# The scale of LayerNorm in the softmax's exponent, and a reordered first block, in a gated cross-attention and SwiGLU kernel

## The reference

```python
def _layernorm(x, axis=-1, eps=1e-05):
    m = jnp.mean(x, axis=axis, keepdims=True)
    v = jnp.var(x, axis=axis, keepdims=True)
    return (x - m) / jnp.sqrt(v + eps)
...
q, k, v = heads(query @ Wq.T), heads(key @ Wk.T), heads(value @ Wv.T)   # 16 heads of 32
scores = jnp.einsum('bhqd,bhkd->bhqk', q, k) * HD ** -0.5
scores = jnp.where(causal[None, None], scores, -1e9)
out = jnp.einsum('bhqk,bhkd->bhqd', jax.nn.softmax(scores, axis=-1), v)
...
x = x + jnp.tanh(g_xattn[0]) * xattn(_layernorm(x), ctx, ctx, Wq, Wk, Wv, Wo)
x = x + jnp.tanh(g_ffn[0]) * ffn(_layernorm(x), w_gate, w_up, w_down)
return x
```

## Time and profile before

| | us |
|---|---|
| median of 3 runs | 894.29 |
| lowest and highest | 893.69, 894.61 |
| the profiled execution: its own time | 893.84 |
| its span, first to last instruction | 892.0 |
| PE busy | 858.7 |
| DVE busy | 655.2 |
| ACT busy | 439.6 |
| POOL busy | 437.0 |

### The profile page before, as it was taken

One profiled execution on the slowest core, in us unless ns is written; L12 is line 12 of the kernel. 1 busy time (PEld: TensorE's weight loads), 2 busy tenths in 40 slices (PEclk: granted clock), 3 DMA queues, 4 the chain that ended last, 5 costly groups with the idle time before them and its releaser, 6 DMA issues.

```text
span 892.0 us, 12923 instructions
## 1 busy us (share of the span) xinstructions
PE 858.7 (96%) x4089; PEld 708.5 (79%) x4089; DVE 655.2 (73%) x1082; ACT 439.6 (49%) x1130; POOL 437.0 (49%) x372
## 2 busy tenths in 40 slices
PE   4979999999999999999999999999999999999997
PEld 2758888888888878778888888888888888888876
DVE  3777868685868697759878758698487787487782
ACT  2566646555565656546326446055364165361450
POOL 5375767675767665338324615144444146141250
PEclk9999999999999999999999999999999999999999
DMA  6526364555556531537614336333256133243212
GB/s 202 152 63 202 126 206 140 189 168 162 167 163 199 190 123 54 205 120 281 227 41 154 113 120 240 113 115 139 88 195 241 37 129 131 89 157 144 83 42 96
DMA packets 61845, 129.53 MB, mean 145 GB/s; under 512 B 8672, under 2 KB 21472, under 8 KB 61792
## 3 DMA queue, kind: packets, MB, share of 16 engines
q1 hardware_dynamic: 61504, 128.85, 42.6%
q10 hardware_dynamic: 288, 0.00, 0.0%
HBM read 100.72 MB, written 27.80 MB: 144 GB/s over the span
## 4 chain that ended last, share of the span: by engine, by line
PE 79%; POOL 6%; DVE 6%; ACT 4%; issue 3%; DMA 1%; SPq 0%; ACTq 0%; POOLq 0%; DVEq 0%
PE psum L1723 34%; PE psum L1475 24%; PE psum L1773 18%; POOL xs L561 4%; PE psum L1509 3%; POOL e L575 2%; ACT e L791 1%; PE psum L1590 1%; ACT pT L762 1%; DMA wq_stage<-wq_t 1%; DVE pT L1017 1%; DVE den L1071 1%; POOL hT L697 1%; DVE aT L1033 1%; ACT aT L779 1%
## 5 line engine op out<-in xcount | busy, mean ns | idle before, releaser
L1723 PE MATMUL psum<-xv,ring 128*128 128x512 f32 x1344 | 308.0, 390 | 0.9 <-ACT a L934 0.7
L1723 PEld LDWEIGHTS psum<-xv,ring 128*128 128x128 f32 x1344 | 251.3, 188 | 55.1 <-ACT a L934 1.1
L697 POOL TENSOR_TENSOR hT<-th,hT 128x512 fp32r<-128x512 f32 x48 | 86.7, 1806 | 200.7 <-ACT hT L954 200.7
L1773 PE MATMUL psum<-w_d,hT 128*128 128x512 f32 x768 | 177.7, 390 | 1.3 <-POOL hT L697 0.8
L1773 PEld LDWEIGHTS psum<-w_d,hT 128*128 128x128 f32 x768 | 143.6, 188 | 32.7 <-POOL hT L697 2.0
L575 POOL TENSOR_TENSOR e<-e,rden 128x616 f32<-128x616 f32 x64 | 78.0, 1220 | 103.4 <-DVE rden L1073 77.0
L1475 PE MATMUL psum<-xT,wq 128*128 128x512 f32 x384 | 95.6, 402 | 3.5 <-POOL xT L567 2.9
L1475 PE MATMUL psum<-wo,aT 128*128 128x512 f32 x384 | 95.4, 398 | 0.5 <-DVE aT L1033 0.5
L1355 DVE SCALAR_TENSOR_TENSOR acc<-psum,gate_ffn,acc 128x512 f32<-128x512 f32 x64 | 47.6, 749 | 65.1 <-PE psum L1773 65.1
L922 ACT ACTIVATE a<-psum 128x512 f32<-128x512 f32 x48 | 28.7, 599 | 131.6 <-PE psum L1723 131.4
L1475 PEld LDWEIGHTS psum<-xT,wq 128*128 128x128 f32 x384 | 71.4, 191 | 18.9 <-POOL xT L567 3.1
(11 more groups left out here) (107 smaller groups left out, 1231.4 us busy)
## 6 DMA issues: line engine op xcount, KB each, us to landing
ring<-w_var SPq DMA_DIRECT2D x48, 896.0 KB, 4.6
w_var<-stage SPq DMA_DIRECT2D x12, 896.0 KB, 5.0
x_ln<-x SPq DMA_DIRECT2D x32, 256.0 KB, 4.9
x_res<-x SPq DMA_DIRECT2D x32, 256.0 KB, 5.2
x_mid<-x_res SPq DMA_DIRECT2D x32, 256.0 KB, 2.0
x<-x_mid SPq DMA_DIRECT2D x16, 512.0 KB, 5.6
acc<-x_mid SPq DMA_DIRECT2D x16, 512.0 KB, 6.0
out<-acc SPq DMA_DIRECT2D x32, 256.0 KB, 2.0
```

Source lines behind the costliest of these rows:

```text
L697: nc.gpsimd.tensor_tensor(hT[:, 1, i % HH, j, :], h[:, :], hT[:, 0, i % HH, j, :].bitcast(f32), ALU.subtract).then_inc(h_lo, 1)
L1723: last = nc.tensor.matmul(psum[:, bank, :], stat, mov, start=start and j == 0, stop=j == len(terms) - 1, skip_group_check=not start)
L1773: last = nc.tensor.matmul(m_bank[t % 2][:, :], hT[:, a, m, t // TT, (t % TT) * P:(t % TT + 1) * P], w_d[:, HH * h + m, :], start=m == 0 an ...
```

## The change

Four things are done. `rstd` no longer touches x. It is computed as (HD * var + HD * EPS) ** -0.5, which is LayerNorm's scale times SCALE, and it becomes the `scale` operand of `exp0` and `exp1`, one value per partition, in the place of the constant SCALE; `nmx` is the maximum times the same value, negated. The DMAs to and from `rs_row`, `rsb`, and `x_scale` go, and `x_high_t` waits for the load alone. `exp0` and the first `nmx` of a block wait for `scale_ready`.

Block 0 is formed in the same way: its queries come from `x_t`, so that normalising, transposing and splitting rows of x go. The loads of `xs` and `wq_stage` are issued first, half of them from ACT's queue. 24 products of `ident` with itself (`WARM`) run on PE before the mean of Wq, whose four products now wait each for its own part of Wq.

The program of block 0 on each engine is written anew. PE scores the first unit of tile t + 1 ahead of the second unit of tile t; keys 0 and 1 come before queries 2 and 3. DVE takes the statistics of block 0 there and those of block 1 in place of block 2. Block 1 takes those of blocks 2 and 3, two per place in place of one.

POOL splits the output weights (`wo`) and the values of the second batch after block 0's probabilities. `v_late`, the second half of `v_full`, lies over other memory, and SP therefore waits for `v_split[1]` before it fetches the weights of the second stage and the rows `x_res` of block 1's residual. NEG becomes -1e30.

```diff
-    NEG = -1e9
+    NEG = -1e30
+    WARM = 24
@@ SP @@
-            load_x(0, first=True)
-            for k in range(KD):
-                sp.dma_start(wq_stage[:, k, :], ...)
+            for k in range(KD // 2):
+                sp.dma_start(xs[:, k, :], xt_f[0, :, k, :]).then_inc(xs_in[k], 16)
+            for k in range(KD // 2):
+                sp.dma_start(wq_stage[:, k, :], ...)
             ctx_stage; wk_stage
+            load_x(0, first=True)
             wv_stage
-            sp.wait_ge(t_full, 4)
-            load_x(1, first=True)
+            load_xs(1)
             x_res <- wo_t
-            load_xs(1, first=True)
-            spread_rstd(1, first=True)
+            load_x(1)
...
             load_xs(2)
+            load_x(2)
             sp.wait_ge(wo_split, 2)
+            sp.wait_ge(v_split[1], 1)
             fetch(1, 0)
             fetch(1, 1)
@@ POOL @@
-            def x_scale(n):
-                pool.wait_ge(rsb_in, 16 * n)
-                for k in range(KD):
-                    pool.wait_ge(xs_in[k], 16 * n)
-                    nc.gpsimd.tensor_tensor(xs[:, k, :], xs[:, k, :], rsb[:, :], ALU.mult).then_inc(x_scaled, 1)
+            def variance(n): rstd = mv * HD + HD * EPS
+            def score_scale(n):
+                if not (isinstance(n, int) and n == 0):
+                    pool.wait_ge(exp1_done, 4 * n)
+                pool.wait_ge(var_eps, n + 1)
+                nc.gpsimd.tensor_tensor(q_scale[:, :], rstd[:, :], half[:, :], ALU.pow).then_inc(scale_ready, 1)
+            variance(0); score_scale(0)
+            x_low_t(1, (0, 1)); probabilities(0, 0); x_low_t(1, (2, 3))
+            probabilities(0, 1); probabilities(0, 2); probabilities(0, 3)
+            variance(1); score_scale(1)
+            wo low parts, then v_low_rows(1)
             def block(n, ahead, first=False):
                 probabilities(n, 0)
-                x_scale(n + 1)
                 x_low_t(n + 1, (0, 1))
...
                 probabilities(n, 3)
+                score_scale(n + 1)
                 if ahead:
-                    rstd1(n + 2)
+                    variance(n + 2)
@@ ACT @@
+            for k in range(KD // 2, KD):
+                act.dma_start(xs[:, k, :], xt_f[0, :, k, :]).then_inc(xs_in[k], 16)
+            for k in range(KD // 2, KD):
+                act.dma_start(wq_stage[:, k, :], ...)
             def x_high_t(n, k):
-                act.wait_ge(x_scaled, 4 * (n - 1) + k + 1)
+                act.wait_ge(xs_in[k], 16 * n + 16)
-                nc.scalar.activation(e[:, t % 2, 0:UH, :], ..., ACT.Exp, scale=SCALE)
+                nc.scalar.activation(e[:, t % 2, 0:UH, :], ..., ACT.Exp, scale=q_scale[:, t:t + 1])
-                        bias=nmx[:, t % 2, h:h + 1], scale=SCALE, accum_out=...)
+                        bias=nmx[:, t % 2, h:h + 1], scale=q_scale[:, t:t + 1], accum_out=...)
+            first_block(): exp0(0, 0) query0(3) x_high_t(1, 0..3) wo_high(0) exp1(0, 0) exp0(0, 1)
+                p(0, 0) p(0, 1) exp1(0, 1) p(0, 2) wo_high(1) exp0(0, 2) p(1, 0) exp1(0, 2) p(1, 1)
+                p(1, 2) exp0(0, 3) q(0) p(2, 0) exp1(0, 3) q(1) p(2, 1) p(2, 2) v_high(0) q(2) ...
@@ DVE @@
+            x_low_t(0..3); centre and wq_low in turn; query0(0) query0(1) k_low(0) k_low(1)
+            stats(0, 0..3); query0(2)
+            first_block(): shift0(0, 0) k_low(2) k_low(3) query0(3) denominator0(0, 0) shift0(0, 1)
+                shift1(0, 0) denominator1(0, 0) v_copy(0) denominator0(0, 1) p(0, 0) shift1(0, 1) p(0, 1)
+                denominator1(0, 1) p(0, 2) shift0(0, 2) p(1, 0) denominator0(0, 2) v_copy(1) shift1(0, 2)
+                p(1, 1) denominator1(0, 2) p(1, 2) shift0(0, 3) denominator0(0, 3) q(0) p(2, 0)
+                shift1(0, 3) q(1) p(2, 1) stats(1, 0) stats(1, 1) denominator1(0, 3) p(2, 2) q(2)
+                v_low_rows(0) p(3, 0) p(3, 1) stats(1, 2) stats(1, 3) q(3) p(3, 2)
@@ PE @@
+            for _ in range(WARM):
+                nc.tensor.matmul(t_bank[0][:, 0:P], ident[:, :], ident[:, :], start=True, stop=True)
             avg product, each of the four waiting for its own wq_in[k]
+            queries 0 and 1, k by k, each k waiting for w_split k + 1
+            keys(0) keys(1) query(2, 2) keys(2) keys(3)
+            first_block(): unit(0, 0) query(3, 3) unit(1, 0) unit(0, 1) batch_values(0) p(0, 0)
+                unit(1, 1) p(0, 1) p(0, 2) unit(2, 0) p(1, 0) batch_values(1) unit(2, 1) p(1, 1) p(1, 2)
+                unit(3, 0) q(0) p(2, 0) unit(3, 1) q(1) p(2, 1) p(2, 2) q(2) p(3, 0) p(3, 1) q(3) p(3, 2)
```

More of the change, by code:

```diff
@@ L90, in t_base @@
     def t_base(n):
[L91 removed]
+        return 12 * n
     V_AT = 4
@@ L815, in step, with query0 @@
-            def step(n, first, query):
+            for k in range(KD):
+                x_high_t(0, k)
+            for k in range(KD):
+                split_hi(wq_centred, wq[:, 0, k], wq_stage[:, k, :], k + 1)
+            act.wait_ge(gates_in, 32)
+            nc.scalar.activation(gate_t[:, :], gates[:, :], ACT.Tanh).then_inc(gates_tanh, 1)
+            def query0(m):
+                m_high(m, m, qT[:, 0, m, :])
+            query0(0)
+            query0(1)
+            act.wait_ge(k_zero, 1)
@@ new lines, in _, with first_block, p, q @@
+            k_high(0)
+            k_high(1)
+            query0(2)
+            k_high(2)
+            k_high(3)
+            def first_block():
+                def p(t, r):
+                    p_high(0, t, r, 3 * t + r)
+                def q(m):
+                    m_high(M_Q1 + m, m, qT[:, 0, m, :])
+                exp0(0, 0)
+                query0(3)
+                for k in range(KD):
+                    x_high_t(1, k)
+                wo_high(0)
+                exp1(0, 0)
+                exp0(0, 1)
+                p(0, 0)
+                p(0, 1)
+                exp1(0, 1)
+                p(0, 2)
+                wo_high(1)
+                exp0(0, 2)
+                p(1, 0)
+                exp1(0, 2)
+                p(1, 1)
+                p(1, 2)
+                exp0(0, 3)
+                q(0)
+                p(2, 0)
+                exp1(0, 3)
+                q(1)
+                p(2, 1)
+                p(2, 2)
+                v_high(0)
+                q(2)
+                p(3, 0)
+                p(3, 1)
+                q(3)
+                p(3, 2)
+                v_high(1)
@@ L832, in step @@
-                q_at = M_Q1 if first else m_base(n) + 8
+                weighted(0)
+                exp1(n, 0, lambda: weighted(1))
+                weighted(2)
+                weighted(3)
+                if query:
+                    for k in range(KD):
+                        x_high_t(n + 1, k)
+                q_at = m_base(n) + 8
                 def q(m):
@@ new lines, in step @@
+                st(3)
+                if not query:
+                    xv_low(0, B11, b11_at)
+                q(1)
+                q(2)
+                p(3, 0)
+                q(3)
+                p(3, 1)
+                p(3, 2)
+                if not query:
+                    form(0, T1)
+            first_block()
+            step(1, True, True)
+            with dve.Fori(2, NB - 2) as n:
+                step(n, True, True)
+            step(NB - 2, True, False)
+            step(NB - 1, False, False)
```

607 lines of the change are left out of this document (281 added, 326 removed).

## The result

The changed kernel takes 899.26 us (898.39 to 900.95, four runs) against 894.28 for the kernel before: a ratio of 1.0058, with a 95% interval of 1.0046 to 1.0070. The forecast of 899.2 stood on the right side and on the right number. The number came by luck: held against the traces, the sum had the price of the operand 4.5 us too small and everything else 4.7 us too dear, and the two errors cancel.

A forecast was written before the change was run, and what follows sets the result against it. It took block 0 as bound by the chain through the engines, later blocks by PE with one gap. Block 0 +4.5, block 1 +2.6, blocks 2 to 6 -3.0, block 7 +0.8: +4.9, so 899.2 us; range 889.5 to 903.

The forecast's parts named there:

- the gap that goes in the steady blocks: Blocks 2 to 6: PE's 0.92 us wait for a low part before its third round of transposes goes without x_scale.
- the three waits at the end of block 0: Block 0, tiles 2 and 3: PE stands 2.5, 2.4 and 3.0 us before p(2, 0), p(3, 0) and p(3, 1).
- I take 0.05 a piece: ACT's exponentials: the per-partition scale adds 0.05 us each, bounds 0 and 0.08; 0.4 us per exp1.
- I take back 0.3 of the 0.92: Blocks 2 to 6: longer exp1 delays queued copies, leaving 5 x (-0.6) = -3.0 us.
- the 1.28 of the earlier trace: Block 7: a PE wait of 1.28 us behind an exp1, for which the forecast put +0.8 us (0 to +1.2).
- Rival 1: All blocks: the scale operand costs nothing; +0.3 us in all, 894.6 us; chance 0.18.
- 5 x 0.92 = 4.6: Blocks 2 to 6: us saved as the 0.92 us gap goes in each, before the operand's price.
- The walk gives 0.3, 0.5, 0.9 and 1.2 us at four places: Block 1: PE waits from doubled statistics and a late low part of q(3), 4.0 us in all; +2.6 taken.
- the walk: Start and block 0, step by step by engine: block 1's scores at 76.8 us at price zero, 78.5 with 0.05.
- one term of 1.6 us: End of block 0: one loss to PE's lowered clock behind the new gaps, 1.6 us added.
- Rival 3: Last query and block 1's start: clock stays at half, twice the 1.6, operand at 0.08; 903.1 us; chance 0.12.
- Rival 2: Block 0, tiles 2 and 3: queued steps overlap, gaps sum to less than 6 us; 889.6 us; chance 0.27.

The follow-up runs named there:

- experiment 1: The changed kernel with the constant SCALE back as scale of both exponentials, leaving LayerNorm's scale out of the attention's exponent: 890.13 us, 0.9951 of the kernel before.
- experiment 9: The changed kernel with clock-holding products behind Wq's mean, statistics behind the second sum and the copy p(1, 1) ahead of tile 2's exp1: 895.66 us.
- experiment 3: The kernel before with only LayerNorm's scale put into the exponent for blocks 1 to 7, old start and old block 0 kept: 890.81 us, 0.9958.
- experiment 6: The changed kernel with 8 more products of ident behind Wq's mean, while PE waits for centred Wq: 898.30 us, 1.0047 of the kernel before.
- experiment 7: The changed kernel with block 0's second sum and low part p(2, 2) ahead of two statistics of block 1 on DVE: 897.27 us, 1.0037.
- experiment 4: The kernel of experiment 3 with ACT's high parts of block 1's x before the first exp0, POOL's low parts around the first probabilities: 888.58 us, 0.9931.
- experiment 5: The changed kernel without the 24 warm-up products ahead of Wq's mean (WARM = 0): 900.03 us, 1.0056 of the kernel before.

## Why the prediction was right, and where only its sum was

**What held and what was luck.** Right were the side, the gap that goes in the steady blocks, and the three waits at the end of block 0, each in its place. The total was luck: with 0.09 in place of 0.05 the same sum would have had some 4 us more, near 903, at the edge of its range. Of the signs that it named, the mean of the second-half activations was 0.427 (0.39 to 0.40 forecast), their steps 0.39 (0.35), block 1's first scores came at 81.33 (near 80) behind a window at clock 0.51 (0.50), and Wq's mean was done at 12.24 (13.8).

**The operand's size: too small.** The step "I take 0.05 a piece" is wrong: 0.09, above the upper bound of 0.08, and the section "What ACT_TABLE_LOAD costs" of the page "ScalarE: Activation LUTs" of the Trainium skill was right where the bounds from the earlier trace rows were not. These took the length of an activation without an operand from a slope through two other shapes; a group of like activations with the operand and one without it give the price directly (427 and 341 ns).

**Where the operand is paid.** The step "I take back 0.3 of the 0.92" for each steady block put the price where it costs little (0.14 to 0.21 in blocks 2 to 5). It put too little where it is paid: 0.3 in block 6 (measured 1.69), 0.5 in block 1 (1.61), 0.8 in block 7 (1.64), 1.7 in block 0 (3.44). In block 7 it also had the wrong wait: the 1.28 of the earlier trace rows did not grow, those of the scores for `exp1` did. In all the sum had 4.6 us for the operand and the runs show 9.1. Rival 1, the free operand, falls at both ends: the operand is not free, and without it the time is 890.1 and not 894.6.

**Everything else: too dear.** At price zero the sum had +0.3 us, and experiment 1's cuts show -4.4.
- Blocks 2 to 6: "5 x 0.92 = 4.6" is short of the measured 7.1. In block 6 of before two more waits for DVE, of 0.43 and 0.49, stood behind the first, and these go too: 2.26. In the other four 1.2 goes each, where the gap was 0.92; the rest, 0.3, lies within PE's busy time (41.86 before, 41.56 to 41.59 in experiment 1, in blocks 2 and 3). Half of that came with the changed kernel (41.71) and half with the constant scale. What makes PE's busy time longer beside a busier ACT or POOL was not settled.
- Block 1: +2.1 forecast, +0.36 measured. "The walk gives 0.3, 0.5, 0.9 and 1.2 us at four places" was right in its places (0.35, 0.34, 0.87, 0.71 in the kernel after), but half of it comes only together with the operand: experiment 1 keeps 0.35 and 0.70.
- Block 0: +2.8 at price zero with the clock's share, +2.25 measured. The order of the walk held; the terms of the operand, the start and the clock were mis-sized.

**The start.** The mean was done at 12.24, below the range of 12.9 to 15.6, since the warm-up itself ended at 8.8 and not at 10.4. The queries then ended at 21.65 where the walk had 21.4. The gap behind the mean was in the walk (2.1, measured 2.26). What was missed is the clock behind it: the queries took 7.15 us and not 5.5, which took back the 1.6 us that the earlier mean had given.

**The clock** was one term of 1.6 us behind the new gaps. The query behind them lost 1.35 against the 3.00 of the earlier trace rows, another at 63.56, behind the wait of 3.07, took 4.18 and lost 1.2, and the first two lost the 1.6 just named: 4.2 in three places. Rival 3, twice this and 903.1, did not come: from 81 to 85 the granted clock was 1.00 again.

**Rival 2** said that steps queued one behind the other would overlap, and fell: the gaps before `p(2, 0)`, `p(3, 0)` and `p(3, 1)` sum to 7.1 us, above the 6 that it needed, and in experiment 9 gains at different links gave more than the best of them. It was right in one thing: in blocks 2 to 5 the operand's price does fall away. That the price-free kernel of experiment 1 lands near its 889.6 has another cause, the steady blocks.

**The cause of the whole.** The scale in the exponent is worth having (-0.4%, experiment 3) even at 0.09 us a piece; the loss is in the new start and order of blocks 0 and 1, 8.5 us. Experiments 6 and 7 show two of its causes, the clock after the mean and the statistics ahead of the second sum, and the three edits of experiment 9 win back 3.6 us by the medians. The rest was not taken apart; above all no run gave block 1 its single statistics back in the new order, where it takes 3.44 us more than in experiment 3.

## What to carry to other kernels

Price an operand by the start-to-start steps of a row of like instructions, and then ask in each stage which engine's queue is late and whether a longer wait lets the clock fall: the same 0.09 us cost 1.6 us a block behind POOL's product, 0.15 once that was gone, and 1.6 again in the blocks with doubled statistics. A right total can hide two wrong terms, so cut both traces at the same places and hold each term of the sum against its own cut. A change of several parts is best run part by part: here one part was worth -0.4%, and the other cost 1%. And before a difference at the start of a kernel is put down to an edit, look whether steps that the edit leaves alone took the same time.

## What the runs showed of the hardware

- The 48 matmuls of the warm-up, alike in each kernel, took 6.97 us in one profiled execution (experiment 1), 7.10 in another (after) and 8.11 in a third (experiment 6). The eight matmuls of Wq's mean behind an idle PE took 6.67 (before), 6.39 (experiment 4) and 5.10 (experiment 3). What stands behind them in block 0 is moved by 1 to 1.6 us for no cause in the kernel; cuts of block 0 from single executions are no better than that.
- Idle time of 2.26 us on PE behind 3.60 us at full clock brought the granted clock to 0.76 over the next 7.15 us (after); with eight products in that time it stayed at 1.00 (experiment 6).
- The column of the granted clock says 1.00 from 7.41 to 14.00 in experiment 5, while the eight matmuls in it take 0.82 us each, where the same ones take 0.45 in the kernel after. It says 1.00 from 10 to 17 in the kernel before too, where they take 0.83. In these stretches, ahead of its first change in the execution, the length of a matmul tells the clock and the column does not:

```profile
7.41:14.00 6.59, 6.55 (x8) 2.44 (x8) 1.33 (x3) 0.09 (x1) 2.23 (x2) 1.00 0.98 324
```
